# Attention A scores as two 64-query halves side by side, and a token order to match

## The chip, the cores and the metric

The kernel runs on one core of one Trainium2 chip. The metric is device time in microseconds (us), here the median of three runs of the kernel before: 951.85 us (951.2 to 951.88). One execution was also profiled; that one took 950.79 us.

## The reference, cut to what matters

The program is one pass through four residual blocks on x of shape (2, 512, 512): attention A, a mixture of 8 low-rank experts, attention B, and the experts again, each on a layer norm of x. Only attention A's scores are touched by the change, and, through the order of the tokens, what reads or writes x at the two ends.

```python
# attention A: 32 query heads, 8 key/value heads, head size 128, s = 512 tokens, b = 2
q = hidden_states @ _dequant(q_codes, q_scales)        # then rotary position encoding
k = hidden_states @ _dequant(k_codes, k_scales)
v = hidden_states @ _dequant(v_codes, v_scales)
causal = jnp.tril(jnp.ones((s, s), dtype=bool))
mask = jnp.where(causal, 0.0, -jnp.inf)
scores = jnp.einsum('bhqd,bhkd->bhqk', q, k) * scale + mask[None, None]
attn = jax.nn.softmax(scores, axis=-1)
out = jnp.einsum('bhqk,bhkd->bhqd', attn, v)
```

The mask is causal: a query sees no key behind itself.

## The kernel before, in words

Each engine has its own hand-written program (the `block.*` functions), and semaphores tie them together. There is no planner: the order in which the lines stand is the order in which an engine does its work. TensorE's program is the one that matters here.

Attention A runs over 8 key/value heads `j`. For each there are 8 slots `s`: 4 query heads times 2 sequences of 512 tokens. So `scores(j, s, ...)` is called 64 times. Between two calls TensorE projects queries, keys or values (`project`, lines 1253 to 1255), multiplies probabilities by values (`a_pv`, lines 1372 to 1374) and multiplies by the output weights (`a_out`, again through lines 1253 to 1255). The first key/value head has its own order (`first_group`); heads 1 to 6 go through a hardware loop of three passes, two heads a pass; the last one is written out and followed by `tail`.

Numbers are split in a high and a low 16-bit part, so every product is three matmuls: high by high, high by low, low by high. One call of `scores` takes the 512 queries in four tiles `i` of 128, in the order 3, 0, 2, 1 (`A_ORDER`). Tile `i` needs keys 0 to (i+1)*128, so its three matmuls (lines 1352, 1353, 1354) stream 512, 128, 384 and 256 columns. Each is a full 128 by 128 array: 128 head elements by 128 queries. The results go to PSUM banks 0 or 1 (tile 3), 2 (tiles 0 and 2) and 3 (tile 1, and the row sums at column 256). Before tile 0 the call waits for `plo_done`: VectorE must have read the previous slot's probabilities out of bank 2.

VectorE's `a_max` (line 1964) then adds the mask and takes the row maximum of each tile in one instruction, in the same order of tiles; ScalarE takes the exponential in place (`a_exps`, line 989), VectorE the reciprocal of the row sum, and ScalarE and VectorE write the probabilities as high and low parts (lines 1025 and 1981). SyncE turns them by a DMA (`turn_head`), and `a_pv` uses them one slot later or more.

In attention B there are matmuls that don't use the whole array. `b_scores` and `b_keys` (lines 1640, 1622, 1666) contract over 64 rows, two at a time in the upper and the lower half of the rows. `b_pv` (line 1734) makes 32 output rows for each of four heads, four at a time in four strips of 32 columns. Its operands are 32-bit, and such a product shows as two matmul records in the trace.

At the start SyncE issues the loads in a row (line 475 and on); `mask` is one of three constants that VectorE waits for (line 2118) ahead of its first rotary step. At the end each finished tile of x is sent out by one DMA of 128 rows (line 575).

Of the kernel before, what the change touches and what calls it, by code (L numbers as in the profile page):

```python
# [15 lines left out]
F32 = mybir.dt.float32  # L16
F16 = mybir.dt.float16
BF16 = mybir.dt.bfloat16
I32 = mybir.dt.int32
U32 = mybir.dt.uint32  # L20
ALU = mybir.AluOpType
# [3 lines left out]
P = 128  # L25
B, S, D = 2, 512, 512
TOK = B * S
NT = TOK // P
ST = S // P
# [17 lines left out]
LOWEST = -3e38  # L47
# [13 lines left out]

A_ORDER = (3, 0, 2, 1)
PROB_ORDER = (0, 2, 1, 3)
A_BANK = {0: (2, 0), 2: (2, P), 1: (3, 0)}
SUMS_AT = 2 * P

# [38 lines left out]
LN_BANK = {0: (0, 1, 0, 1, 6, 1, 6, 6), 2: (2, 3, 2, 3, 2, 3, 2, 3)}  # L105
# [106 lines left out]
def build(nc, t_in, out):  # L212
    ctx = ExitStack()
    with ctx:
        def sb(name, shape, dt):
            return ctx.enter_context(nc.sbuf_tensor(name, shape, dt))
# [5 lines left out]
        bank = [banks[:, i] for i in range(8)]  # L222


        x = sb("x", [P, NT, D], F32)
# [2 lines left out]
        xn = sb("xn", [P, 2, D], F32)  # L228
        rows = sb("rows", [P, 2, 2, D], F16)
        ident = sb("ident", [P, P], F32)  # L230
        mask_f = sb("mask_f", [P, P], F32)
        mask_w = sb("mask_w", [P, S], BF16)
        mask_b = mask_w[:, S - P:S]
        cos_b = sb("cos_b", [P, ST, B_HD // 2], F32)
        sin_b = sb("sin_b", [P, ST, 2, B_HD // 2], F32)
        iota_e = sb("iota_e", [P, EXPERTS], F32)
# [62 lines left out]
        cos_a = sa("cos_a", [P, S], F32)  # L299
# [8 lines left out]
        rt2 = sa("rt2", [P, 2, S], F32)  # L308
        arena = sa("arena", [P, 10 * 1024], F32)
        scn = arena[:, 0:sum(QUANT_COLS.values())]  # L310
        q_hi = arena[:, 0:2048].bitcast(F16).rearrange("p (s n) -> p s n", s=8)
        q_lo = arena[:, 2048:4096].bitcast(F16).rearrange("p (s n) -> p s n", s=8)
        ctx_hi = arena[:, 4096:6144].bitcast(F16).rearrange("p (s n) -> p s n", s=8)
# [142 lines left out]
        def m_place(ph, t):  # L456

            n = NT * ph + t
            return n % 3, 16 * (n // 3 + 1)

        def rows_landed(c, t):

            return 16 * (HALF * (c // 2) + t // 2 + 1)

        block = ctx.enter_context(nc.Block())
        N_CONST = 3


        @block.sync
        def _(sp):  # L470
# [6 lines left out]
            load_scales(sp, "q", 0)  # L477
            for dst, src in ((cos_a, "cos_a"), (sin_a, "sin_a"), (mask_f, "mask")):
                sp.dma_start(dst[:], t_in[src]).then_inc(d_const, 16)
            sp.dma_start(x[:, ST:NT, :], x_in[:, ST:NT, :]).then_inc(d_x[ST], 16)  # L480
            load_codes(sp, "o", 0)
            load_scales(sp, "o", 0)
# [88 lines left out]
            for t in range(NT):  # L571
                if t + 3 < NT:
                    turn_hidden(1, t + 3)
                sp.wait_ge(y_added, NT + B * ST + t + 1)
                sp.dma_start(o_out[:, t, :], x[:, t, :]).then_inc(d_out, 16)
            sp.wait_ge(d_out, 16 * NT)


        @block.gpsimd
        def _(pool):  # L580
# [3 lines left out]
            pool.iota(iota_e[:], pattern=[[1, EXPERTS]], base=0, channel_multiplier=0,  # L584
                      allow_small_or_imprecise_dtypes=True).then_inc(consts, 1)
            pool.memset(mask_w[:, 0:S - P], 0.0).then_inc(consts, 1)
            pool.wait_ge(consts, 4)

            def ln_rsqrt(c, t):
# [660 lines left out]
        def _(pe):  # L1250
# [6 lines left out]
            def ln_t(c, t):  # L1257
                pe.wait_ge(xn_ready, NT * c + t + 1)
                if t >= 2:
                    pe.wait_ge(xt_done, NT * c + t - (c > 0 or t != NT - 1))  # L1260
                for k in range(KT):
                    mm = pe.transpose(bank[LN_BANK[c][t]][:, k * P:(k + 1) * P],
                                      xn[:, t % 2, k * P:(k + 1) * P], ident[:])
                mm.then_inc(xt_ps, 1)

# [63 lines left out]
            def scores(j, s, first, zeros_to=None):  # L1329


                b = s // GROUP
                n = 8 * j + s
                if s == 0:
                    pe.wait_ge(rot_done, 10 * j + ROT_OF[PROJ_AT["k", 0]] + 1)
                if s == 4:
                    pe.wait_ge(rot_done, 10 * j + ROT_OF[PROJ_AT["k", 1]] + 1)
                pe.wait_ge(rot_done, 10 * j + ROT_OF[PROJ_AT["q", s]] + 1)
                for i in A_ORDER:
                    bk, o = a_bank(i, s)  # L1340
                    w = (i + 1) * P
                    if i == 3 and not (first and s < 2):
                        pe.wait_ge(plo_done, 4 * (n - 1))
                    if i == 0 and zeros_to is not None:
                        keep_busy(zeros_to, 8)
                    if i == 0 and not (first and s == 0):
                        pe.wait_ge(plo_done, 4 * (n - 1) + 2)
                    if i == 1 and not (first and s == 0):
                        pe.wait_ge(plo_done, 4 * (n - 1) + 3)
                    o_ap = bank[bk][:, o:o + w]  # L1350
                    qs = slice(i * P, (i + 1) * P)
                    pe.matmul(o_ap, q_hi[:, s, qs], k_hi[:, b, 0:w], start=True, stop=False)  # L1352
                    pe.matmul(o_ap, q_hi[:, s, qs], k_lo[:, b, 0:w], start=False, stop=False)  # L1353
                    mm = pe.matmul(o_ap, q_lo[:, s, qs], k_hi[:, b, 0:w], start=False, stop=True)  # L1354
                    if i != 0:
                        mm.then_inc(s_ps, 1)

            def a_pv(j, kind, s, ring_j, place):
                b = s // GROUP
# [177 lines left out]
            def turn(m, src, ready, count):  # L1537

                pe.wait_ge(ready, count)
                if m >= NT + 2:  # L1540
                    pe.wait_ge(mt_done, m - 1)
                bk = bank[MT_BANK[m % 2]]
                for k in range(KT):
                    mm = pe.transpose(bk[:, k * P:(k + 1) * P], src[:, k * P:(k + 1) * P], ident[:])
                mm.then_inc(mt_ps, 1)

            def second(m, name, first=True, last=True):
# [281 lines left out]
        def _(dve):  # L1829
# [126 lines left out]
            def a_max(j, s):  # L1956

                n = 8 * j + s
                for c, i in enumerate(A_ORDER):
                    bk, o = a_bank(i, s)  # L1960
                    if i != 2:
                        dve.wait_ge(s_ps, 3 * n + {3: 1, 0: 2, 1: 3}[i])
                    dve.nop(nofuse=True)
                    dve.tensor_tensor_reduce(bank[bk][:, o:o + (i + 1) * P], bank[bk][:, o:o + (i + 1) * P],  # L1964
                                             mask_w[:, S - (i + 1) * P:S], 1.0, LOWEST, ALU.add, ALU.max,
                                             smax[:, s % 2, c:c + 1]).then_inc(smax_done, 1)

            def row_factors(j, s):
# [151 lines left out]
            ln_factor(ST)  # L2120
            ln_stats(0, ST + 1)
            dve.tensor_copy(mask_b, mask_f[:])
            rope(0, ("q", 0))
            ln_factor(ST + 1)
            dve.wait_ge(first_hi, FIRST_HIGH.index("q3") + 1)
# [270 lines left out]

def constants():

    pos = np.arange(S, dtype=np.float32)
    inv = (np.float32(1.0) / np.float32(10000.0) ** (np.arange(0, A_HD, 2, dtype=np.float32) / np.float32(A_HD)))  # L2400
    f = pos[:, None] * inv.astype(np.float32)[None, :]
    cos, sin = np.cos(f).T.astype(np.float32), np.sin(f).T.astype(np.float32)

    cos_a = np.concatenate([cos, cos]) * np.float32(PROJ_DN)
    sin_a = np.concatenate([sin, -sin]) * np.float32(PROJ_DN)

    theta, factor, hi, lo, ctx_len = 500000.0, 32.0, 4.0, 1.0, 1024
    idx = np.arange(0, B_HD, 2, dtype=np.float32) / np.float32(B_HD)
    freq = np.float32(1.0 / (2.0 * np.pi)) * (np.float32(theta) ** (-idx)).astype(np.float32)
    scaled = np.where(freq < lo / ctx_len, freq / np.float32(factor), freq)  # L2410
    smooth = np.clip((ctx_len * freq - np.float32(lo)) / np.float32(hi - lo), 0.0, 1.0).astype(np.float32)
    mid = (1 - smooth) * (freq / np.float32(factor)) + smooth * freq
    freq = np.where((freq >= lo / ctx_len) & (freq <= hi / ctx_len), mid, scaled).astype(np.float32)
    phase = (np.float32(2.0 * np.pi) * pos)[:, None] * freq[None, :]
    table = lambda a: np.ascontiguousarray(
        (a.astype(np.float32) * np.float32(ROPE_DN_B)).reshape(ST, P, -1).transpose(1, 0, 2))
    sin_b = table(np.concatenate([-np.sin(phase), np.sin(phase)], axis=1)).reshape(P, ST, 2, B_HD // 2)
    i = np.arange(P)
    mask = np.where(i[None, :] <= i[:, None], 0.0, MASKED).astype(np.float32)
    eye, none = np.eye(64), np.zeros((64, 64))  # L2420
    last = none.copy()
    last[63] = 1.0
    ahead = mask[:64, :64].astype(np.float64)
    weights = [[eye, none], [last, eye * (1.0 - last)]]
    factors = [ahead, ahead + MASKED * last]
    half = np.concatenate([w for pair_ in weights for w in pair_] + factors, axis=1)
    sel = np.tile(half, (2, 1)).astype(np.float32)
    return {"ident": np.eye(P, dtype=np.float32), "mask": mask, "cos_a": cos_a.astype(np.float32),
            "sin_a": sin_a.astype(np.float32), "cos_b": table(np.cos(phase)), "sin_b": sin_b, "sel": sel}


# [45 lines left out]
```

## Time and profile before

| | us |
|---|---|
| median of 3 runs | 951.85 |
| lowest, highest | 951.2, 951.88 |
| the profiled execution's own time | 950.79 |
| its span in the profile | 949.1 |
| TensorE matmuls busy | 912.1 (96%) |
| VectorE busy | 771.8 (81%) |
| GpSimd busy | 618.9 (65%) |
| ScalarE busy | 598.8 (63%) |

The span is the stretch from the first to the last profiled instruction; the execution's own time has 1.7 us around it. Busy time of an engine is the union of its instructions. A matmul's recorded duration is longer than the time it holds the engine: the next one starts before the end of the one ahead. So the difference of two starts tells what a matmul costs, and the duration doesn't. The granted TensorE clock is 0.995 of full speed over the span.

### The profile page before, as it was taken

Reading aid. Unit: us, or ns where it says so; the run is one execution under the profiler, and the core shown is the slowest. Engines: PE = TensorE matmul, PEld = TensorE weight load, DVE = VectorE, ACT = ScalarE, POOL = GpSimd, SP = SyncE. Lnnn points to the kernel's source line nnn. Section 1 sums busy time; section 2 is a strip of 40 time slices with the busy share of each in tenths; the row PEclk is TensorE's granted clock in tenths of the full one; section 3 lists DMA queues with packets and bytes.
Section 4 is the critical chain, followed back from the end, with each engine's and each line's share of the span. In section 5 each row is a group of like instructions: output and inputs, shape, how many; then the busy total and the mean of one; then the engine's idle time right before and its main releaser. Section 6 shows DMA issues by size and latency. Waiting matters only on the chain.

```text
span 949.1 us, 19791 instructions
## 1 busy us (share of the span) xinstructions
PE 912.1 (96%) x6698; PEld 487.6 (51%) x6698; DVE 771.8 (81%) x1812; ACT 598.8 (63%) x1323; POOL 618.9 (65%) x668
## 2 busy tenths in 40 slices
PE   5889999999999999999999999999999989999998
PEld 3445555555555555545555555554445534444543
DVE  6888887887887788788788878898878879996764
ACT  4677666676667567666576756646463469997331
POOL 4788876968777687687777777822368744553211
PEclk9999999999999999999999999999999999999999
DMA  9177376484665556647557465464332943121145
GB/s 339 51 182 173 87 185 145 63 211 107 122 186 88 144 116 157 144 86 199 117 101 190 83 144 144 87 175 84 76 82 55 163 80 64 42 43 24 23 86 159
DMA packets 256005, 114.10 MB, mean 120 GB/s; under 512 B 244144, under 2 KB 244784, under 8 KB 251312
## 3 DMA queue, kind: packets, MB, share of 16 engines
q1 hardware_dynamic: 246416, 70.42, 39.1%
q10 hardware_dynamic: 9504, 42.49, 12.9%
q8 instruction: 60, 0.98, 0.4%
q14 instruction: 25, 0.20, 0.1%
HBM read 49.84 MB, written 2.10 MB: 55 GB/s over the span
## 4 chain that ended last, share of the span: by engine, by line
PE 76%; DVE 10%; ACT 6%; issue 3%; DMA 3%; POOL 1%; SPq 1%; ACTq 0%; DVEq 0%; POOLq 0%
PE bank L1253 16%; PE bank L1255 16%; PE bank L1254 16%; PE bank L1734 4%; PE bank L1352 3%; PE bank L1354 3%; PE bank L1353 3%; PE bank L1372 3%; PE bank L1374 3%; PE bank L1373 3%; ACT bank L989 2%; PE bank L1666 2%; DVE bw_hi L1981 2%; DVE bank L1964 2%; PE bank L1640 2%
## 5 line engine op out<-in xcount | busy, mean ns | idle before, releaser
L622 POOL TENSOR_TENSOR rt<-rt 128x512 f32<-128x512 f32 x80 | 101.6, 1273 | 131.8 <-DVE rt L1949 131.8
L1981 DVE SCALAR_TENSOR_TENSOR bw_hi<-bank,rden,bw_hi 128x128 f16<-128x128 f32 (+3 forms) x256 | 123.3, 544 | 60.9 <-ACT bw_hi L1025 60.9
L989 ACT ACTIVATE bank<-bank,shift,c_score 128x128 f32<-128x128 f32 (+3 forms) x256 | 147.3, 605 | 2.1
L1964 DVE CUSTOM_DVE_ANT_0 bank<-bank,mask_w 128x512 f32<-128x512 f32 (+3 forms) x256 | 117.9, 520 | 21.5 <-PE bank L1354 21.5
L1025 ACT ACTIVATE bw_hi<-bank,rden 128x128 f16<-128x128 f32 (+3 forms) x256 | 114.5, 535 | 22.4 <-DVE rden L1974 22.2
L984 ACT ACTIVATE shift<-smax,c_score 128x4 f32<-128x4 f32 x64 | 19.0, 297 | 155.4 <-DVE smax L1964 155.4
L629 POOL TENSOR_TENSOR arena<-rt,arena 128x512 f16<-128x512 f32 x80 | 92.4, 1158 | 8.6 <-ACT arena L973 7.8
L1253 PE MATMUL bank<-xt,wq_hi 128*128 128x512 f16 x256 | 97.0, 379 | 0.0
L1254 PE MATMUL bank<-xt,wq_hi 128*128 128x512 f16 x256 | 97.0, 379 | 0.0
L1255 PE MATMUL bank<-xt,wq_lo 128*128 128x512 f16 x256 | 97.0, 379 | 0.0
L1253 PE MATMUL bank<-wo_hi,arena 128*128 128x512 f16 x256 | 97.0, 379 | 0.0
L1254 PE MATMUL bank<-wo_lo,arena 128*128 128x512 f16 x256 | 97.0, 379 | 0.0
L1255 PE MATMUL bank<-wo_hi,arena 128*128 128x512 f16 x256 | 97.0, 379 | 0.0
L1006 ACT ACTIVATE pt<-bank,c_score_b 128x512 f32<-128x512 f32 x128 | 79.6, 684 | 15.2 <-PE bank L1666 13.1
L1352 PE MATMUL bank<-arena 128*128 128x512 f16 (+3 forms) x256 | 73.4, 300 | 7.1 <-DVE bw_hi L1981 6.8
L1372 PE MATMUL bank<-bw_lo,arena 128*128 128x512 f16 (+3 forms) x256 | 76.6, 299 | 1.9 <-DMA bw_lo<-bw_hi 1.4
L1373 PE MATMUL bank<-bw_lo,arena 128*128 128x512 f16 (+3 forms) x256 | 76.6, 299 | 0.0
L1353 PE MATMUL bank<-arena 128*128 128x512 f16 (+3 forms) x256 | 76.6, 299 | 0.0
L1354 PE MATMUL bank<-arena 128*128 128x512 f16 (+3 forms) x256 | 73.8, 299 | 0.0
L1374 PE MATMUL bank<-bw_lo,arena 128*128 128x512 f16 (+3 forms) x256 | 73.3, 299 | 0.0
L1947 DVE TENSOR_TENSOR rt<-bank,sin_a 64x512 f32<-64x512 f32 x80 | 55.5, 693 | 16.6 <-PE bank L1255 14.7
L973 ACT ACTIVATE arena<-rt 128x512 f16<-128x512 f32 x80 | 51.3, 645 | 9.9 <-POOL rt L622 9.9
(241 smaller groups left out, 2453.6 us busy)
## 6 DMA issues: line engine op xcount, KB each, us to landing
qcode<-in_q_codes ACTq DMA_DIRECT2D x7, 1024.0 KB, 5.0
qscale<-in_q_scales ACTq DMA_DIRECT2D x7, 1024.0 KB, 7.2
ocode<-in_o_codes ACTq DMA_DIRECT2D x7, 1024.0 KB, 4.9
oscale<-in_o_scales ACTq DMA_DIRECT2D x7, 1024.0 KB, 7.9
kvcode<-in_k_codes ACTq DMA_DIRECT2D x8, 256.0 KB, 7.5
kvcode<-in_v_codes ACTq DMA_DIRECT2D x8, 256.0 KB, 7.9
kvscale<-in_k_scales ACTq DMA_DIRECT2D x8, 256.0 KB, 8.1
kvscale<-in_v_scales ACTq DMA_DIRECT2D x8, 256.0 KB, 8.9
```

The source lines that it names most:

```text
L989: act.activation(a_rows(i, s), a_rows(i, s), ACT.Exp, bias=shift[:, s % 2, c:c + 1], scale=c_score[:, 0:1], accum_out=bank[3][:, SUMS_AT + ...
L1025: act.activation(p_row[:, s % 2, HI_AT[i]:HI_AT[i] + P_STEP * i + 1:P_STEP], turned_back(i, s), ACT.Copy, scale=rden[:, s % 2, c:c + 1]).t ...
L1253: pe.matmul(out_ap, a_hi, b_hi, start=(k == 0), stop=False)
L1254: pe.matmul(out_ap, a_hi, b_lo, start=False, stop=False)
L1255: return pe.matmul(out_ap, a_lo, b_hi, start=False, stop=(stop and k == n - 1))
L1352: pe.matmul(o_ap, q_hi[:, s, qs], k_hi[:, b, 0:w], start=True, stop=False)
L1353: pe.matmul(o_ap, q_hi[:, s, qs], k_lo[:, b, 0:w], start=False, stop=False)
L1354: mm = pe.matmul(o_ap, q_lo[:, s, qs], k_hi[:, b, 0:w], start=False, stop=True)
L1372: pe.matmul(o_ap, v_hi[:, b, vs], hi, start=(kt == 0), stop=False)
L1373: pe.matmul(o_ap, v_hi[:, b, vs], lo, start=False, stop=False)
L1964: dve.tensor_tensor_reduce(bank[bk][:, o:o + (i + 1) * P], bank[bk][:, o:o + (i + 1) * P], mask_w[:, S - (i + 1) * P:S], 1.0, LOWEST, ALU. ...
L1981: dve.scalar_tensor_tensor(out=p_row[:, s % 2, LO_AT[i]:LO_AT[i] + P_STEP * i + 1:P_STEP], in0=turned_back(i, s), scalar=rden[:, s % 2, c: ...
```

## The change

`scores` no longer makes one matmul per tile and term but two, each with 64 of the tile's 128 queries. One writes PSUM partitions 0 to 63 and the other 64 to 127 of the same columns. The half with the earlier 64 queries streams 64 keys fewer: `i*128 + 64` against `(i+1)*128`. In tiles 3 and 2 the earlier queries go to partitions 0 to 63. In tiles 0 and 1 (`SWAPPED`) they go to 64 to 127. So each half of the partitions gets two long and two short tiles. The columns that a short half leaves out keep what stood in PSUM before, and the mask covers them.

Since queries of tiles 0 and 1 then stand exchanged by halves, the tokens of x stand so too in these tiles: the host hands x over in that order, the transposes behind the layer norms ahead of both attentions (`ln_t`) put them in order as they write to PSUM, those of attention B's result (`turn`) exchange them again, `a_max` uses a second mask with its halves exchanged, and the output goes out by two DMAs of 64 rows a tile instead of one of 128. One constant more is loaded and converted. In the very first call, eight small matmuls with zeros clear banks 2 and 3. `s_ps` counts 6 a call and not 3.

```diff
+SWAPPED = (0, 1)
-        mask_f = sb("mask_f", [P, P], F32)
+        back_w = sb("back_w", [P, 2 * P], BF16)
+        mask_f, back_f = arena[:, 4096:4096 + P], arena[:, 4096 + P:4096 + 2 * P]
+        def in_order(a, t):
+            return a.rearrange("p (f n) -> p f n", f=2)[:, ::-1] if t % ST in SWAPPED else a
-        N_CONST = 3
+        N_CONST = 4
+            sp.dma_start(back_f, t_in["mask_back"]).then_inc(d_const, 16)
...
-                sp.dma_start(o_out[:, t, :], x[:, t, :]).then_inc(d_out, 16)
-            sp.wait_ge(d_out, 16 * NT)
+                for f in range(2):
+                    r = (1 - f if t % ST in SWAPPED else f) * P // 2
+                    sp.dma_start(o_out[f * P // 2:(f + 1) * P // 2, t, :], x[r:r + P // 2, t, :]).then_inc(d_out, 16)
+            sp.wait_ge(d_out, 2 * 16 * NT)
+            pool.memset(back_w[:, 0:P], 0.0).then_inc(consts, 1)
...
-                    mm = pe.transpose(bank[LN_BANK[c][t]][:, k * P:(k + 1) * P],
+                    mm = pe.transpose(in_order(bank[LN_BANK[c][t]][:, k * P:(k + 1) * P], t),
                                       xn[:, t % 2, k * P:(k + 1) * P], ident[:])
...
-                    o_ap = bank[bk][:, o:o + w]
-                    qs = slice(i * P, (i + 1) * P)
-                    pe.matmul(o_ap, q_hi[:, s, qs], k_hi[:, b, 0:w], start=True, stop=False)
-                    pe.matmul(o_ap, q_hi[:, s, qs], k_lo[:, b, 0:w], start=False, stop=False)
-                    mm = pe.matmul(o_ap, q_lo[:, s, qs], k_hi[:, b, 0:w], start=False, stop=True)
-                    if i != 0:
-                        mm.then_inc(s_ps, 1)
+                    if first and s == 0 and i in SWAPPED:
+                        for c0 in range(0, S, P):
+                            pe.matmul(bank[bk][:, c0:c0 + P], mask_w[:, 0:P], mask_w[:, 0:P], start=True, stop=True)
+
+                    halves = [(i * P + f * P // 2, (1 - f if i in SWAPPED else f) * P // 2, i * P + (f + 1) * P // 2)
+                              for f in range(2)]
+                    terms = ((q_hi, k_hi), (q_hi, k_lo), (q_lo, k_hi))
+                    for k, (qa, ka) in enumerate(terms):
+                        for q0, r0, keys in halves:
+                            mm = pe.matmul(bank[bk][r0:r0 + P // 2, o:o + keys], qa[:, s, q0:q0 + P // 2],
+                                           ka[:, b, 0:keys], start=(k == 0), stop=(k == len(terms) - 1))
+                            if i != 0 and k == len(terms) - 1:
+                                mm.then_inc(s_ps, 1)
...
-                    mm = pe.transpose(bk[:, k * P:(k + 1) * P], src[:, k * P:(k + 1) * P], ident[:])
+                    mm = pe.transpose(in_order(bk[:, k * P:(k + 1) * P], m), src[:, k * P:(k + 1) * P], ident[:])
...
-                        dve.wait_ge(s_ps, 3 * n + {3: 1, 0: 2, 1: 3}[i])
+                        dve.wait_ge(s_ps, 6 * n + {3: 2, 0: 4, 1: 6}[i])
                     dve.nop(nofuse=True)
+                    mask = back_w[:, (1 - i) * P:2 * P] if i in SWAPPED else mask_w[:, S - (i + 1) * P:S]
                     dve.tensor_tensor_reduce(bank[bk][:, o:o + (i + 1) * P], bank[bk][:, o:o + (i + 1) * P],
-                                             mask_w[:, S - (i + 1) * P:S], 1.0, LOWEST, ALU.add, ALU.max,
+                                             mask, 1.0, LOWEST, ALU.add, ALU.max,
...
             dve.tensor_copy(mask_b, mask_f[:])
+            dve.tensor_copy(back_w[:, P:2 * P], back_f[:])
```

## Rows read from the trace of the kernel before

**Rows 1.** The page: busy time by engine, and the chain that ended last.
```profile
PE 912.1 (96%) x6698; PEld 487.6 (51%) x6698; DVE 771.8 (81%) x1812; ACT 598.8 (63%) x1323; POOL 618.9 (65%) x668
PE 76%; DVE 10%; ACT 6%; issue 3%; DMA 3%; POOL 1%; SPq 1%; ACTq 0%; DVEq 0%; POOLq 0%
```
**Rows 2.** Windows: stretch, its us, busy us (count) by engine, clock, DMA share, GB/s.
```profile
0.00:79.00 79.00, 61.26 (x394) 34.76 (x395) 60.56 (x158) 50.18 (x107) 57.19 (x60) 0.98 0.60 180
79.00:645.00 566.00, 562.91 (x3622) 310.51 (x3619) 465.99 (x1158) 368.11 (x924) 418.44 (x350) 1.00 0.59 136
```
**Rows 3.** Waits of PE in 79 to 645 us: total us, times, longest.
```profile
PE bank L1352 <- DVE bw_hi L1981: 2.7, 6, 1.0
```
**Rows 4.** Timeline of PE, one call of scores: start, us, line, shapes.
```profile
303.50 0.38 PE L1352 MATMUL bank<-arena 128*128 128x512 f16 x1
303.72 0.38 PE L1353 MATMUL bank<-arena 128*128 128x512 f16 x1
...
304.15 0.22 PE L1352 MATMUL bank<-arena 128*128 128x128 f16 x1
...
304.32 0.33 PE L1352 MATMUL bank<-arena 128*128 128x384 f16 x1
...
304.80 0.27 PE L1352 MATMUL bank<-arena 128*128 128x256 f16 x1
...
305.13 0.38 PE L1253 MATMUL bank<-xt,wq_hi 128*128 128x512 f16 x1
```
**Rows 5.** Timeline of PE where the array is divided otherwise than just before.
```profile
751.21 0.27 PE L1255 MATMUL bank<-bw_hi,xt 128*128 128x256 f16 x1
751.41 0.28 PE L1640 MATMUL bank<-kt_b,qt_b 64*128 64x256 f16 x2
...
751.73 0.19 PE L1622 MATMUL bank<-sel 64*128 64x64 bf16 x2
751.86 0.39 PE L1253 MATMUL bank<-bw_hi,xt 128*128 128x512 f16 x1
752.08 0.38 PE L1254 MATMUL bank<-bw_lo,xt 128*128 128x512 f16 x1
...
875.19 0.38 PE L1255 MATMUL bank<-bw_hi,mt 128*128 128x512 f16 x1
875.50 0.64 PE L1734 MATMUL bank<-pt,bv 128*32 128x512 f32 x4
```
**Rows 6.** Timeline of PE around one b_pv, in two narrow windows.
```profile
801.66 0.39 PE L1666 MATMUL bank<-qt_b,kt_b 64*128 64x512 f16 x2 [1.16 <-DMA qt_b<-rows]
801.98 0.64 PE L1734 MATMUL bank<-pt,bv 128*32 128x512 f32 x4
...
802.43 0.61 PE L1734 MATMUL bank<-pt,bv 128*32 128x512 f32 x4
802.98 0.39 PE L1666 MATMUL bank<-qt_b,kt_b 64*128 64x384 f16 x4
```
**Rows 7.** Groups of PE by form, b_pv: busy us, mean ns, idle before.
```profile
L1734 PE MATMUL bank<-pt,bv 128*32 128x512 f32 x128 | 17.0, 605 | 0.0
L1734 PE MATMUL bank<-pt,bv 128*32 128x128 f32 x128 | 6.7, 282 | 0.0
```
**Rows 8.** Timeline of PE around a 3-column transpose.
```profile
684.69 0.38 PE L1255 MATMUL bank<-lora_a_hi,xt 128*128 128x512 f16 x1
684.90 0.27 PE L1592 MATMUL bank<-ident,amax_w 128*3 128x128 f32 x1
685.01 0.17 PE L1253 MATMUL bank<-gate_hi,xt 128*128 128x8 f16 x1
```
**Rows 9.** Timeline of DVE at the start and in the first call.
```profile
21.79 0.68 DVE L1847 BATCH_NORM_STATS2 bn<-x 128x6 f32<-128x512 f32 x1
...
26.14 0.23 DVE L2122 CAST mask_w<-mask_f 128x128 bf16<-128x128 f32 x1
...
34.09 0.70 DVE L1964 CUSTOM_DVE_ANT_0 bank<-bank,mask_w 128x512 f32<-128x512 f32 x1 [0.35 <-PE bank L1354]
...
34.74 0.30 DVE L1964 CUSTOM_DVE_ANT_0 bank<-bank,mask_w 128x128 f32<-128x128 f32 x1
...
35.85 0.69 DVE L1847 BATCH_NORM_STATS2 bn<-x 128x6 f32<-128x512 f32 x1
```
**Rows 10.** Timeline of SP: an input load at the start, an output at the end.
```profile
8.38 0.67 SPq L480 DMA_DIRECT2D x<-in_x  x1
...
937.03 0.57 SPq L575 DMA_DIRECT2D out<-x  x1
```
**Rows 11.** DMA issues by transfer: count, KB each, median us to landing.
```profile
out<-x SPq DMA_DIRECT2D x8, 256.0 KB, 2.4
x<-in_x SPq DMA_DIRECT2D x1, 1024.0 KB, 12.9
```

## What is predicted

> **What bounds the kernel now.** I read the page's busy shares and chain first, then the windows by stage, then TensorE's waits, and last the timeline of single calls. The page gives TensorE 96% of the span and 76% of the chain that ended last [rows 1]. Heads 1 to 7 and the end of head 0 of attention A fill 79 to 645 us. There TensorE is busy for 562.91 of 566.00 us, while VectorE has 465.99 and the others less [rows 2]. The one wait worth a line is for VectorE's probabilities, 2.7 us in six places [rows 3]. So in this stretch a TensorE nanosecond is a nanosecond of the kernel, whichever way it goes. Ahead of 79 us it is different: TensorE is busy for 61.26 of 79 us [rows 2], and VectorE, ScalarE and GpSimd take turns in holding up the rest.
>
> One call of `scores` runs from 303.50 to 305.13, 1.63 us, without a gap [rows 4]. The starts show what one matmul costs: 0.216 us for 512 columns (303.50 to 303.72), 0.056 for 128 (three of them from 304.15 to 304.32), 0.162 for 384, 0.11 for 256. That is 0.42 ns a column. The 3 x 1280 = 3840 columns of a call make 1.61 to 1.63 us. Of the 64 calls, 57 lie in the stretch that TensorE bounds (head 0 from slot 5: 3, heads 1 to 6: 48, the last head to slot 5: 6).
>
> **What the call saves.** With the halves in two column strips of the array, each strip gets 448 or 512, 64 or 128, 320 or 384, 192 or 256 columns a term. With tiles 0 and 1 exchanged both come to 448+128+320+256 = 1152, and 512+64+384+192 = 1152. Three terms are 3456 columns, 384 fewer than now: 384 x 0.42 = 0.16 us a call. This holds only if the strips run at the same time and each goes on without waiting for the other. The nearest row is `b_pv`: four 32-column strips. All four first records fit in 0.64 us from 801.98, and one lasts 0.605 in the mean, so they start within some 0.03 us and run side by side [rows 6, 7]. The second record of each product comes only at 802.43 [rows 6], 0.45 us later. The code issues head by head, and yet the first records of heads 2 to 4 were not kept back until head 1's second had started. So work for a free strip passes an earlier piece that waits for a busy one. That is what the exchange needs: one strip ends tile 3 by 192 columns (0.08 us) ahead of the other. I take the strips as independent, with 0.01 us lost where more than one piece would have to be passed.
>
> **What the call adds.** Line 1255 at 751.21 streams 256 columns, 0.11 us, and would be followed at 751.32; line 1640, with the rows in two halves, starts at 751.41. The way back: two pairs of 64 columns from 751.70 leave the array at about 751.76, and line 1253 starts at 751.86. Full array to column strips: 875.19 plus 0.216 is 875.41, and line 1734 starts at 875.50. From row halves to column strips: 801.66 plus 0.22 is 801.88, start at 801.98. Column strips to row halves: the second four start at 802.43 and stream for 0.43, and line 1666 starts at 802.98 [rows 5, 6]. Five kinds of change, and each costs 0.09 to 0.10 us over the stream. I found the same at every such place of attention B. The first matmul into column strips is then itself some 0.02 longer: 0.45 from 801.98 to 802.43, against 0.43 for 1024 column times (two for each of the 512 columns of these 32-bit operands) [rows 6]. Every call of `scores` stands between products with the full array, so it pays twice: 0.10 + 0.02 going in, 0.10 coming out: 0.22 in all.
>
> A call is then 1.63 - 0.16 + 0.22 + 0.01 = 1.70 us, 0.07 longer. Times 57: +4.0 us. The bounds of this one term: 0.03 a call (0.19 for the two changes and nothing else, +1.7) and 0.11 (some waiting for weights or for each other in the short products, +6.3). I take 0.07 since it goes by the 16-bit and the column rows together. The 24 weight loads instead of 12 cost nothing by themselves: in `b_pv` eight loads and eight matmuls go by without lengthening the stream.
>
> The six waits of 2.7 us [rows 3] don't pay for it: VectorE's work on slot s starts when tile 3 is there and is wanted at tile 0 of slot s+1, and this interval only grows by a call's 0.07. I take back 0.4.
>
> **The rest, step by step.**
> - First call (33.13 us): eight zero matmuls of 128 columns, 8 x 0.056 = 0.45, in two lots that use the full array between strips: four more changes, 0.4, and the 0.22. VectorE waits for TensorE here: its mask and maximum of tile 3 starts at 34.09 after 0.35 idle, of tile 0 at 34.74, and it is busy without a gap behind 35.85 [rows 9]. Tile 0 is released by tile 2's matmuls, which end some 0.6 later than now (0.12 in, 0.1 out, 0.22 zeros, 0.12 in, less 0.03): VectorE gets it at about 35.2, and passes on 0.5. Bounds 0 (the group's later waits swallow it) and 1.0. I take 0.5. The other six calls outside the stretch that TensorE bounds: `keep_busy` or a wait covers them in most; 0.2 (0 to 0.6).
> - Start: one load more on SyncE's queue ahead of the rest of x. Such an issue takes 0.67 [rows 10]; x issued at 8.38 landed 12.9 later [rows 11], at 21.3, and is wanted at 21.79 [rows 9], so up to 0.2 is late. One conversion more on VectorE, 0.23 [rows 9], 0.12 of it over its neighbour. GpSimd then holds the chain, so I take 0.2 (0 to 0.5). GpSimd's extra memset lies in idle time before 8 us.
> - Transposes that write 64-column halves in exchanged order: the same columns on the same array; no row shows such an order of output. 0 taken, -0.1 to +0.5.
> - Output: two issues of 64 rows, each 0.57 or less [rows 10], of which the second is behind the first. Its transfer is half as long (2.4 us to landing for 256 KB [rows 11]), so +0.1 (0 to 0.5). The doubled issues of the other tiles lie in SyncE's idle time between tiles, some 2.6 us.
> - `a_max` with the other mask: the same shapes, 0. Two increments a tile, 0.
>
> Sum: 4.0 - 0.4 + 0.5 + 0.2 + 0.2 + 0.1 = **+4.6 us**. The profiled execution took 950.79, so 955.4 by it; the median of the runs stands 1.06 above it, so 956.4.
>
> **Rivals.**
> 1. In order (0.20). The strips run at once, but matmuls start in program order, and where a strip is free the next one for it stands behind one for the busy strip. Then tile 3 ends with the longer half (1536 columns), tile 0 costs 384, tile 2 1152, tile 1 768: 3840, nothing saved. A call is 1.63 + 0.22 + 0.02 = 1.87, +0.24, times 57 is +13.7, less 1.2 from the six waits, plus 1.0: +13.5, 965.4. For it: all records of before start in their order and halves were always of one length there, so an unequal pair is not shown. Against it: `b_pv`'s second records [rows 6]. The Trainium skill (TensorE: Matmul & The Clock Gate, part 3, "The mechanism") says that matmuls are strictly in order in start and end; by that rule the time is this rival's. A smaller case stands at the forecast's upper end: weight loads that don't keep up. The mean load record is 487.6 / 6698 = 0.073 us [rows 1]; at half of that for half the columns, one at a time, tile 0's six loads hold 0.22 against its 0.16, +0.06 a call and 3.4 us on the forecast, 959.8. The Trainium skill (TensorEngine Tiling, "Restrictions") says that column strips turn the fast weight load off; no run here shows a 64-column load.
> 2. Free change (0.12), the other side. A 64-column strip does not cost the 0.10 on the way in and out, or the weight load hides it. Line 1592, 3 columns wide, starts at 684.90, 0.216 behind line 1255, and line 1253 follows at 685.01: a narrow product with no change paid [rows 8]. A call is then 1.63 - 0.16 + 0.02 = 1.49; 57 x -0.14 = -8.0, plus 1.0 for the rest: -7.0, 944.8. It decides from below 0.08 a change: there the call breaks even. Against it are the products of line 1734 and 1640, which are no transposes and all pay [rows 5, 6].
> 3. No overlap (0.03): the halves run one after the other, 2304 x 3 columns a call, 2.9 + 0.2 us: 57 x 1.5 = +85, 1037. `b_pv` speaks against it.
> 4. Near zero (0.05): half of the gain of rival 2, or more of the start and the waits absorbed: within 2 us of before.
>
> **How the numbers follow.** Forecast 0.60: 956.4, its own range 953.9 (0.03 a call and little else) to 959.4 (0.11 and the upper ends). About 0.2%, 1.9 us, is what a measurement can tell from no change: 949.9 to 953.8. Faster 0.13 (rival 2 and a little of 4), same 0.07, slower 0.80. The range for 8 in 10 goes from 952.8 to 966.5: it takes in the forecast, most of rival 1 and the edge of 4, and leaves out rivals 2 and 3.
>
> **What would show it.** TensorE's timeline of one call: start to start of the calls' neighbours 1.70 and not 1.63; a gap of 0.10 ahead of the first and behind the last of the 24 products; in tile 0 the long half starts before the short half of its pair (right), or never before 1536 columns are through (rival 1). Windows: 79 to 645 grows by 3.6. VectorE's maximum of tile 0 in the first call is 0.5 later. The forecast is wrong if the change of layout isn't seen in the starts, or if the call is longer than 1.75 or shorter than 1.65.

## The result and the profile after

The changed kernel takes 955.03 us (median of 7 runs, 953.86 to 957.77) against 951.85 of before. The ratio is 1.0045, with a 95% interval of 1.0028 to 1.0061, so it is slower by some 4.3 us (2.7 to 5.8); the two medians alone are 3.2 apart. The forecast was +4.6 and 956.4. The profiled execution, at 957.77, was the slowest of the seven; what sets it apart is told below.

The page after: busy time by engine, and the chain of work that ended last, as in [rows 1].
```profile
PE 919.7 (96%) x7474; PEld 499.6 (52%) x7474; DVE 773.4 (81%) x1813; ACT 599.2 (63%) x1323; POOL 619.3 (65%) x669
PE 80%; DVE 9%; ACT 3%; DMA 3%; issue 2%; SPq 1%; ACTq 0%; POOL 0%; DVEq 0%; POOLq 0%
```
TensorE's share of the chain rose from 76 to 80%. One call of `scores` in TensorE's timeline (start, duration, line; the 24 products are one row):
```profile
297.84 0.38 PE L1266 MATMUL bank<-wo_hi,arena 128*128 128x512 f16 x1
298.15 1.67 PE L1370 MATMUL bank<-arena 128*64 128x448 f16 x24
299.75 0.39 PE L1264 MATMUL bank<-xt,wq_hi 128*128 128x512 f16 x1
299.98 0.38 PE L1265 MATMUL bank<-xt,wq_hi 128*128 128x512 f16 x1
```
The last full product ends its stream at 297.84 + 0.216 = 298.06; the first half starts at 298.15, 0.09 to 0.10 later. From 298.06 to 299.75 is 1.69 to 1.70 us; [rows 4] gives 1.63. That is the loss in one picture: a shorter stream between two pauses. A little more is lost right behind it: the next start comes 0.23 later, at 299.98, where such products are 0.22 apart in [rows 4].

Did the strips pass each other? Two windows of 0.05 and 0.02 us show which products were under way in that call, by their records (busy us, mean ns):
```profile
L1370 PE MATMUL bank<-arena 128*64 128x512 f16 x2 | 0.6, 379 | 0.0
L1370 PE MATMUL bank<-arena 128*64 128x448 f16 x1 | 0.4, 352 | 0.0
L1370 PE MATMUL bank<-arena 128*64 128x128 f16 x1 | 0.2, 219 | 0.0
...
L1370 PE MATMUL bank<-arena 128*64 128x512 f16 x1 | 0.4, 379 | 0.0
L1370 PE MATMUL bank<-arena 128*64 128x448 f16 x1 | 0.4, 352 | 0.0
L1370 PE MATMUL bank<-arena 128*64 128x128 f16 x2 | 0.3, 219 | 0.0
L1370 PE MATMUL bank<-arena 128*64 128x64 f16 x1 | 0.2, 193 | 0.0
```
The first three rows are of 298.742 to 298.79: a 128-column half of tile 0 runs and no 64-column one, though the code issues the short half first. At 298.82 to 298.84, in the other four, two long halves have started and one short one. So products start out of the program's order, each strip on its own.

### The profile page after: what moved, and what is told of

Read it like the earlier page. It is cut to its first block, busy times and chain, and to the rows that moved or that the text cites. A ratio compares the mean times of both kernels' runs of the same rounds, so it can differ in the third digit from the quotient of the medians.

```text
span 956.0 us, 21354 instructions
## 1 busy us (share of the span) xinstructions
PE 919.7 (96%) x7474; PEld 499.6 (52%) x7474; DVE 773.4 (81%) x1813; ACT 599.2 (63%) x1323; POOL 619.3 (65%) x669
## 4 chain that ended last, share of the span: by engine, by line
PE 80%; DVE 9%; ACT 3%; DMA 3%; issue 2%; SPq 1%; ACTq 0%; POOL 0%; DVEq 0%; POOLq 0%
PE bank L1264 18%; PE bank L1265 17%; PE bank L1266 17%; PE bank L1370 10%; PE bank L1751 4%; PE bank L1389 3%; PE bank L1390 3%; PE bank L1391 3%; PE bank L1683 2%; PE bank L1657 1%; DMA mt<-m_stack 1%; DVE bw_hi L1999 1%; DMA x<-in_x 1%; PE bank L1273 1%; ACT pt L1017 1%
## 5 line engine op out<-in xcount | busy, mean ns | idle before, releaser
L1370 PE MATMUL bank<-arena 128*64 128x128 f16 (+7 forms) x1536 | 110.3, 290 | 5.7 <-DVE bw_hi L1999 5.3
L1982 DVE CUSTOM_DVE_ANT_0 bank<-bank,mask_w 128x512 f32<-128x512 f32 (+1 forms) x128 | 82.7, 646 | 25.7 <-PE bank L1370 25.7
L1370 PEld LDWEIGHTS bank<-arena 128*64 128x64 f16 x1536 | 80.7, 110 | 40.9 <-DVE bw_hi L1999 17.8
L1966 DVE TENSOR_TENSOR rt<-bank,cos_a 128x512 f32<-128x512 f32 x80 | 55.4, 692 | 1.1
```

Source lines behind the costliest of these rows:

```text
L1370: mm = pe.matmul(bank[bk][r0:r0 + P // 2, o:o + keys], qa[:, s, q0:q0 + P // 2], ka[:, b, 0:keys], start=(k == 0), stop=(k == len(terms) - 1))
```

## The experiments

Each run is compared with the kernel before, on the same chip. Times by head are from the start of VectorE's first maximum in slot 5 of one head to that of the next. In the kernel before such a head takes 78.38 to 78.39 us, and 78.94 and 78.78 where TensorE's loop jumps back. The first of the seven intervals (77.26) and the last (78.92) reach into the two heads with an order of their own.

**The surroundings alone.**
```diff
-                    for k, (qa, ka) in enumerate(terms):
-                        for q0, r0, keys in halves:
...
+                    pe.matmul(o_ap, qh, k_hi[:, b, 0:w], start=True, stop=False)
+                    pe.matmul(o_ap, qh, k_lo[:, b, 0:w], start=False, stop=False)
+                    mm = pe.matmul(o_ap, ql, k_hi[:, b, 0:w], start=False, stop=True)
```
The zeros of the first call are gone too. The kernel leaves out the exchange of the queries in tiles 0 and 1, while the rest still counts on it, so what it computes is not the program's result; it serves for its time alone.

> The changed kernel with its exchanged token order, its second mask, its extra load and its halved output transfers, but with the scores made as before: one matmul of 128 queries per tile and term. The queries of tiles 0 and 1 are not exchanged by halves there, so this leaves that reordering out. Theory (the strips and their two changes of array layout cost the time): a call of scores is 1.63 us again, and the rest is worth +0.2 to +0.5 over the kernel before: 952.0 to 952.4, ratio 1.000 to 1.001. Rival (the surroundings cost it: the extra load ahead of x, the output in halves, transposes that write in exchanged order): 954.5 to 955, ratio 1.003.


Measured: 952.48, ratio 1.0011 (0.9999 to 1.0023). A head takes 78.38 again. The theory holds, and the rival's 1.003 is outside the interval. The middle, +1.0 (-0.1 to +2.2), is above the 0.2 to 0.5 that I gave the surroundings; the last run below puts 0.8 of it at the output.

**Without the exchange.**
```diff
-SWAPPED = (0, 1)
+SWAPPED = ()
```
The zeros of the first call stay as they are.

> The changed kernel with SWAPPED = (): the tokens stay in order, and the earlier 64 queries of every tile go to partitions 0 to 63. One strip then streams 3 x (448+64+320+192) = 3072 columns a call, the other 3 x 1280 = 3840. Theory (strips run independently and the exchange is what lets 384 columns go): the longer strip sets the call, 1.64 + 0.03 + 2 x 0.10 = 1.86 us against 1.70 of the changed kernel, 57 x 0.16 = +9: 964. Rival (the pairs start together anyway, the exchange does nothing): 955, a call of 1.70.


Measured: 962.74, ratio 1.0116 (1.0099 to 1.0134). A call:
```profile
619.50 0.38 PE L1266 MATMUL bank<-wo_hi,arena 128*128 128x512 f16 x1
619.81 1.82 PE L1370 MATMUL bank<-arena 128*64 128x448 f16 x24
621.57 0.39 PE L1264 MATMUL bank<-xt,wq_hi 128*128 128x512 f16 x1
```
1.76 + 0.09 = 1.85, for the 1.86 worked out: the strip with 3840 columns sets it. A head takes 79.87, 1.0 above the changed kernel and not 8 x 0.15 = 1.2, since the wait for VectorE that each head has ahead of one tile 0 (0.22 in the changed kernel) is gone here. The exchange of tokens does what it is made for.

**How much may be passed.**
```diff
-for k, (qa, ka) in enumerate(terms):
-    for q0, r0, keys in halves:
+for q0, r0, keys in halves:
+    for k, (qa, ka) in enumerate(terms):
```


> The changed kernel, but the three terms of one half are issued before the three of the other, so that a piece for the free strip stands behind two that wait for the busy strip. If the engine lets pieces pass over any number of waiting ones, a call stays at 1.70 us and the kernel at 955. If two may wait for a strip before the issue stops, I work out 0.18 more from the columns (1.65 instead of 1.47 of streaming), 57 x 0.18 = +10: 965. If one may wait, 2.08 of streaming, +0.6 a call, 989. If none may (program order, rival 1 of the prediction), 2.5 of streaming, +1.0 a call, over 1010.


Measured: 955.07, ratio 1.0040 (1.0024 to 1.0056). A call:
```profile
613.59 0.38 PE L1266 MATMUL bank<-wo_hi,arena 128*128 128x512 f16 x1
613.90 1.68 PE L1370 MATMUL bank<-arena 128*64 128x448 f16 x24
615.51 0.39 PE L1264 MATMUL bank<-xt,wq_hi 128*128 128x512 f16 x1
```
1.61, hardly above 1.60; a head takes 78.91 to 78.92 for 78.87 to 78.88. Almost nothing is lost though pieces for the free strip stand behind several for the busy one. Rival 1 is out.

**No change of layout around the call.**
```diff
+def strips(out_ap, a, b, start, stop):
+    for f in range(2):
+        h = slice(f * P // 2, (f + 1) * P // 2)
+        mm = pe.matmul(out_ap[h], a[:, h], b, start=start, stop=stop)
+    return mm
... (in words)
-  full products in project, a_pv, a_out, tail_out and the fillers of attention A
+  strips(...) in their place
```


> Every 16-bit product of attention A (projections, probabilities by values, output weights, the fillers) is made in two strips of 64 columns too, so that the array's layout changes only around the few 32-bit transposes of the first head. Theory (the two changes of layout are what turns the call's gain into a loss): a call is 1.48 us and nothing is paid around it: 57 x (1.48 - 1.63) = -8.6 against the kernel before, 943.5 (941 to 946), ratio 0.991. Rival (it is the narrow weight loads and the doubled count of instructions that cost): no gain around the calls, and the 128-column products of the value projection, 48 in each of 16, go from 0.056 to 0.08 or so: +18 or more, 965 to 975.


Measured: 953.35, ratio 1.0027 (1.0011 to 1.0042): neither theory's number. The three full heads without a jump take 77.33 to 77.35, 1.04 less than before, so the gain around the calls is there and the narrow loads don't eat it up. But the two heads with a jump back take 80.56 and 80.68. TensorE's timeline at the first of them:
```profile
263.73 0.39 PE L1271 MATMUL bank<-wo_hi,arena 128*64 128x512 f16 x2
265.81 1.59 PE L1386 MATMUL bank<-arena 128*64 128x448 f16 x21 [1.70 <-DVE bw_hi L2016]
268.90 0.38 PE L1386 MATMUL bank<-arena 128*64 128x256 f16 x3 [1.51 <-issue]
```
1.70 of idle ahead of the first call behind the jump and 1.51 inside it, the second with nothing to wait for. This points at the jump, and the next runs take it away.

**The jump, three times.**
```diff
-with pe.Fori(0, KV_HEADS // 2 - 1) as i:
+for i in range(KV_HEADS // 2 - 1):
...
+pe.wait_ge(invq_done, 1)      # changed and all-strips versions: banks 2 and 3 cleared here, ahead of the
+for k in (2, 3):              # first projection, and no longer in the first call of scores
+    keep_busy(k, 1)
+    pe.matmul(bank[k][:, S - P:S], mask_w[:, 0:P], mask_w[:, 0:P], start=True, stop=True)
```
Two fillers fewer stand ahead of these new ones.

> The kernel before with TensorE's three-pass hardware loop over heads 1 to 6 written out, nothing else. In the profile of before the two heads that hold a jump back take 78.94 and 78.78 us against 78.38 to 78.39 of the others, so 0.96 in all. Theory (the jump back stalls the engine once a pass): 951, ratio 0.999. Rival (the stall is instruction fetch that written-out code pays elsewhere): no difference or up to 1 us slower. It is the control for the next three.

> The changed kernel with TensorE's loop written out and the clearing of banks 2 and 3 moved ahead of the first projection, where TensorE waits for the layer norm. Theory (the call is 0.065 longer and the first call 0.5 to 0.8, the rest is nothing): what is left over the kernel before is 57 x 0.065 = 3.7 and some 0.5 in the first head, less 1.1 for the loop: 951.85 + 3.1 = 955, ratio 1.003. Rival (the jumps back cost more with the longer code, a good part of the changed kernel's loss): 953 or less, ratio 1.001.

> All of attention A's 16-bit products in two strips, as in the run before, with TensorE's loop written out and the clearing of the banks moved as in the run beside it. There the heads without a jump took 77.34 us against 78.38 of the kernel before, those with one 80.56 and 80.68. Theory (the gain was there, and the jump back with twice the instructions gave it back): all six heads take 77.34, 6 x 1.04 = -6.2, the first and the last -1.5, the first group +1: 951.85 - 7 = 945, ratio 0.993. Rival (the engine falls behind in fetching instructions wherever they are twice as many, and the loop's edge only showed it): the written-out heads take 78 or more, ratio 0.998 or above.

| written out | us | ratio | heads, without the last |
|---|---|---|---|
| before | 950.6 | 0.9996 (0.9979 to 1.0013) | first 77.26, then 78.38 to 78.39 |
| changed | 952.64 | 1.0021 (1.0007 to 1.0035) | first 77.92, then 78.86 to 78.87 |
| all in strips | 946.0 | 0.9944 (0.9923 to 0.9966) | 78.12, 78.21, then 77.33 to 77.52 |

The heads with a jump fall to what the others take, in all three. In the time this shows clearly only where the code is twice as long: the kernel before, written out, can't be told from the loop, and the changed one, at 1.0021, lies between theory (1.003) and rival (1.001). What it is in a jump back that costs stays open. All in strips and written out is faster than both kernels: 5.3 us (3.2 to 7.3) below the kernel before. The call there has no pause around it:
```profile
488.28 0.39 PE L1271 MATMUL bank<-wo_hi,arena 128*64 128x512 f16 x2
488.50 1.65 PE L1386 MATMUL bank<-arena 128*64 128x448 f16 x24
489.97 0.61 PE L1271 MATMUL bank<-xt,wq_hi 128*64 128x512 f16 x4
```
1.47 from 488.50 to 489.97, and 488.28 + 0.216 is where it starts. Its first two heads take 0.8 and 0.9 more than the next. That is of this execution and not of the code: the run on the output below, with the same program up to there, has 77.45 and 77.34. In the first of them TensorE waits 0.75 and 0.70 for the DMA that turns the probabilities, against 0.40 and 0.37 there.

**Strips, but every key.**
```diff
-halves = [(i * P + f * P // 2, (1 - f if i in SWAPPED else f) * P // 2, i * P + (f + 1) * P // 2) ...]
+halves = [(i * P + f * P // 2, f * P // 2, w) ...]        # and SWAPPED = ()
```


> The run beside it (all in strips, loop written out), but with the tokens in order and both halves of a tile streaming all (i+1)*128 keys. Theory (strips cost next to nothing, the gain is the 384 columns): a call is 1.63 to 1.64 again, a head 78.4 to 78.6, the kernel 951 to 953, 57 x 0.155 = 8.8 above the run beside it. Rival (the strips themselves make it faster, for instance by loads that overlap better): within 3 us of the run beside it.


Measured: 950.77, ratio 1.0002 (0.9987 to 1.0016); heads 78.40 to 78.43. Strips alone change nothing, and the gain of the run above is that of the 384 columns. It is 5 and not 8.8. A head gives 1.0, not 8 x 0.157 = 1.26, since TensorE's idle ahead of the tile 0 that waits for VectorE is 0.3 there and 0.15 here. The two slow heads there cost 1.5, the first head here some 0.6.

**The output.**
```diff
  # all in strips, written out: the last tile, and others that are not exchanged, in one transfer again
+if t % ST not in SWAPPED:
+    sp.dma_start(o_out[:, t, :], x[:, t, :]).then_inc(d_out, 16)
+    continue
...
  # the kernel before: every tile in two transfers
-                sp.dma_start(o_out[:, t, :], x[:, t, :]).then_inc(d_out, 16)
+                for f in range(2):
+                    r = f * P // 2
+                    sp.dma_start(o_out[r:r + P // 2, t, :], x[r:r + P // 2, t, :]).then_inc(d_out, 16)
```


> The kernel with all of attention A in strips and TensorE's loop written out, but the output of the tiles that are not exchanged (2, 3, 6, 7, the last one among them) in one transfer of 128 rows again. In the traces so far the end of the span lies 3.2 us behind VectorE's last instruction in the kernel before, and 4.0 to 4.4 in the four with halved transfers. Theory (the second issue of the last tile, 0.5 behind the first, ends the kernel): 3.2 to 3.3 again, so 0.8 less: 945.2 against 946.0, ratio 0.9935 to 0.994. Rival (the last landing is set by the queue's earlier transfers): 4.0 still, ratio as in the run without this edit, 0.9944.

> The kernel before with nothing changed but its output, each tile in two transfers of 64 rows. Theory (0.5 for the second issue and 0.3 for the longer single ones): the end of the span 4.0 us and not 3.2 behind VectorE's last instruction, +0.8: 952.7, ratio 1.0008. Rival (half a transfer is over the sooner, as I forecast: +0.1): 3.3 and ratio 1.000. The time alone may not tell these apart, the trace does.


VectorE's last instruction and the page's span, of the changed kernel, of the kernel before with halved output, and of all in strips with its last tile in one transfer:
```profile
951.99 0.75 DVE L2239 SCALAR_TENSOR_TENSOR x<-bank,c_ffn,x 128x512 f32<-128x512 f32 x1 [2.89 <-PE bank L1266]
span 956.0 us, 21354 instructions
```
```profile
947.42 0.75 DVE L2222 SCALAR_TENSOR_TENSOR x<-bank,c_ffn,x 128x512 f32<-128x512 f32 x1 [1.84 <-PE bank L1257]
span 951.5 us, 19799 instructions
```
```profile
937.06 0.75 DVE L2259 SCALAR_TENSOR_TENSOR x<-bank,c_ffn,x 128x512 f32<-128x512 f32 x1 [1.84 <-PE bank L1269]
span 940.2 us, 27755 instructions
```
From the start of that instruction to the end of the span are 4.0, 4.1 and 3.1 us; the kernel before has 949.1 - 945.87 = 3.2. All nine profiles with halves have 4.0 to 4.4, the three with a whole last transfer 3.1 to 3.2. The halves cost 0.8 to 0.9 at the end. The times alone, 944.59, ratio 0.9938 (0.9923 to 0.9953), and 952.39, ratio 1.0006 (0.9993 to 1.0019), lean the same way and don't prove it. Of these two, all in strips is the best version: 5.9 us (4.5 to 7.3) below the kernel before.

## Why the prediction was right, point by point

- **The call.** 0.064 us longer and not 0.07. The two changes of layout cost 0.09 and 0.10 and the stream is 1.50 long: 3456 columns at 1.47, and 0.03 by which the first product of each strip is longer. Not in the sum: each stretch between two calls is 0.010 longer, since the first full product behind a call is (0.23 for 0.22 above). Together 57 x 0.074 = 4.2 for 4.0.
- **The waits.** Five waits for VectorE inside a call, 0.24 to 0.33 each before, are 0.14 to 0.22 now: 0.5 given back, 0.4 foreseen. But the six of [rows 3] were read wrongly: these two of them stand right behind a jump back, in the kernel before:
```profile
264.46 0.39 PE L1352 MATMUL bank<-arena 128*128 128x512 f16 x1 [0.70 <-DVE bw_hi L1981]
...
421.62 0.39 PE L1352 MATMUL bank<-arena 128*128 128x512 f16 x1 [0.55 <-DVE bw_hi L1981]
```
  Written out, the same kernel has none there and the 0.15 of the other heads further on, so most of these two waits goes with the jump and not with VectorE's work.
- **The stretch as a whole.** On TensorE the first and the last of the 57 calls are 549.48 apart before and 553.44 after: 4.0 more, and the forecast had 3.6. That is 56 x 0.074 = 4.1, less 0.5 for the waits, and 0.3 at the two jumps. VectorE's own count from slot 5 of head 0 to slot 5 of head 7 gives 3.7 (637.78 - 84.98 = 552.80 against 630.05 - 80.99 = 549.06). The two spans are 7.0 apart (956.0 and 949.1): 4.0 more lie ahead of this stretch, 3.7 in it, and 0.7 less behind it, though the output's 0.8 is there. Behind it the twelve profiles have 316.0 to 319.8, so that much is spread.
- **The first call.** VectorE spends 1.76 from its first maximum to the statistics behind the last one in [rows 9] (34.09 to 35.85). In the run without the exchange, which has the same zeros, it is 2.23, so +0.47 for the 0.5 forecast; with the zeros moved ahead it is back at 1.77. In the profiled execution of the changed kernel it is 3.13:
```profile
36.78 0.70 DVE L1982 CUSTOM_DVE_ANT_0 bank<-bank,mask_w 128x512 f32<-128x512 f32 x1 [0.89 <-PE bank L1370]
...
39.91 0.69 DVE L1864 BATCH_NORM_STATS2 bn<-x 128x6 f32<-128x512 f32 x1
```
```profile
35.00:40.00 5.00, 5.00 (x38) 2.53 (x37) 2.52 (x11) 3.40 (x4) 4.22 (x5) 0.66 0.02 3
```
  The second fence is TensorE's window of 35 to 40 us. The granted clock there is 0.66 in the mean, so part of it at 1.2 GHz, and that goes with 0.9 over the 2.23. The run half by half shows the same: 0.66 in this window, and 3.42 from 35.47 to 38.89. So of three profiled executions with full-array zeros in the first call two have the low clock there, and of the nine of other kernels none has. Idle time ahead of it doesn't explain it: TensorE had been idle for 2.01 us before the transposes here and for 1.41 in the kernel before, but for 2.02 in the one with halved output and 2.10 in the changed one written out, both with a granted clock of 1.00 in this window. Whether the change brings the low clock to this place stays open; the forecast had no term for it.
  This execution also starts the call late: its first maximum is at 36.78, 34.09 before. 2.15 of these 2.7 are there before the transposes ahead of the call (34.65 against 32.50), the rest is in tile 3, partly at the low clock. In the other profiles the first maximum starts between 33.8 and 35.5, and the kernel before has 35.0 when only its output is changed. What of the 2.7 belongs to the change isn't settled.
- **The start.** 0.2 taken for one load more. The rest of x landed at 21.3 in both profiles. Too small to see, as are the 0.2 of the other six calls.
- **The output.** Mis-sized: 0.8, and I had 0.1 with 0.5 as the upper bound. I let the half transfer be over sooner than a whole one. SyncE issues the second 0.5 behind the first, and it lands 2.35 after its own issue; a whole one took 2.0. The median to landing is 2.4 us for 128 KB and for 256 KB.
- **The jump back.** Not in the sum. The two heads with it hold 0.6 and 0.4 over the others before, and 0.8 and 0.7 after. That difference is no finding: the full-array run has 1.0 and 1.0, and the kernel before with halved output 0.7 and 0.9, with as many products of TensorE as before.
- **Rivals.** Rival 1, program order, fell by the trace itself. The Trainium skill (TensorE: Matmul & The Clock Gate, part 3, "The mechanism") has matmuls strictly in order in start and end; here two 128-column products of one strip start ahead of a 64-column one issued before them for the other, as the windows above show, so the measurement decides. Rival 2, a free change, fell at every one of the 57 calls. The row it rested on is a transpose of 3 columns, which pays in none of the profiles (0.216 ahead of it and 0.11 behind, in all twelve). The smaller case of slow weight loads is not seen: the six products of tile 0 take 0.17 us, as long as their columns, and in the run with every key the strips cost nothing. The Trainium skill (TensorEngine Tiling, "Restrictions") has the fast load turned off in strips; that shows here at most in the record of a load, 0.11 us for 64 columns.

The total hides that the parts were not all right: the output 0.7 too low, and no term for the 0.01 behind each call, the jumps and the clock. The parts with a measurement add up to 4.2 - 0.5 + 0.5 + 0.8 = 5.0, the measured total is 4.3 (2.7 to 5.8). The mechanism and the size of the main term were right; that the total came so near is in part luck, as the noise is larger than most of the small terms.

## What to carry to other kernels

Count a change of how TensorE's array is divided as about 0.1 us each way, as at the places of [rows 5] and [rows 6] and around the 57 calls here, and set it against what the divided stretch saves: 0.16 us a call can't pay for two. If the saving is real, divide the neighbours too, which cost nothing by itself here (78.40 against 78.38 a head), and look at what twice the instructions do at a loop's jump (3.2 to 3.3 us here). At the very end of this kernel, two half transfers were over 0.8 later than one whole.

## What the runs showed that I had not expected

- Two strips of 64 columns run every 16-bit product of attention A at the speed of the full array (a head 78.40 against 78.38), in spite of twice as many instructions.
- A head with a jump back of TensorE's loop takes 0.4 to 1.0 us more with as many products as before, 0.7 to 1.3 with the scores in halves, and 3.2 to 3.3 with twice as many products throughout.
- A piece for a free strip passes at least three that wait for the other. This is worked out: a limit of two would have cost 0.18 a call in the run half by half, and it cost 0.007.
- A wait put down to VectorE (1.70 behind the jump) can be the engine's own: written out, it is gone.
